# Windowed attention on one Trainium2 core: softmax sums applied to the output tile instead of the probabilities

## The chip, the cores and the metric

The kernel runs on one core of one Trainium2 chip. The metric is the device time of one execution in microseconds (us). Engines: PE is TensorE (matmuls; PEld is its weight load, which overlaps them), DVE is VectorE, ACT is ScalarE, POOL is GpSimd, SP is SyncE, which issues most DMAs.

## The reference

Two blocks with residual connections on x of 4 x 1024 x 256 in float32: first a causal attention of 16 heads of 16, then a network of two layers, each with an attention of 8 heads of 64 over windows of 128 tokens and a gated feed-forward part. The part that matters here, for one layer:

```python
q, k, v = split(shift_token(x) @ wqkv)          # 8 heads of 64
q, k = rotary(l2norm(q) * qs, l2norm(k) * ksc)
# window w of 128 queries sees the keys of windows w-1 and w
sim = einsum('bhwid,bhwjd->bhwij', 8 * bq, bk)   # 128 x 256 per head and window
sim = where(mask, -max, sim)
attn = softmax(sim, axis=-1)
out = einsum('bhwij,bhwjd->bhwid', attn, bv)     # 128 x 64 per head and window
x = x + out @ wo
h = layernorm(shift_token(x)) @ w1 + b1
a, g = split(h)
x = x + (a * gelu(g)) @ w2 + b2
```

## The kernel before

The program has two stretches. `prepare`, `causal_attention` and `project_causal` compute the first attention; they end about 890 us into the span and the change does not touch them. `layers` computes the two layers as 8 passes (`it` = 0 to 7, layer times batch), each `attention(it)` followed by `feed_forward(it)`. All five engines have their own hand-written program with the same step counter, and they meet at semaphores (`Count.of(it, item)` is the value that stands for an item).

`attention` has 32 units `u`: window `w = u // 4`, and within a window 4 units of two heads. `place(u, h)` tells at which place (feature tile `p`, and `side`, upper or lower 64 partitions) a head lies. One unit goes through

- PE `scores` (L1322): q times k, two heads side by side into bank `s_ps[u % 2]`;
- DVE `mask_scores` (L1763): adds the band, negates, takes the row minimum, writes `p_sb`;
- ACT `exponentials` (L1535): exp in place in `p_sb`, row sums into `total`;
- DVE `invert_sums` (L1812), then `scale_probs` (L1818): the reciprocal of two sums, and two products that divide the two heads' probabilities in `p_sb`;
- PE `turn_probs` (L1387): transposes the 128 x 128 blocks into `pt_ps`, so that keys lie on partitions; it waits for `scaled`;
- ACT `copy_probs` (L1551): `pt_ps` to `p_t`;
- PE `values` (L1402), once for two units: with v as the 128 x 64 stationary operand, the output with features on partitions goes to `o_ps`. One head's 64 features use one half of the array's columns (`tile_position=(0, side * HD2)`), and the two halves alternate;
- ACT `copy_output` (L1559), once for a window: `o_ps` to `o_t`.

PE's program for step u is, in this order: `scores(u)`, `turn_probs(u-2)`, in the first two steps of a window `turn(w+1, 0)` and `turn(w+1, 1)` (L1308, the rotated q and k of the next window, transposed into `turn_ps`, from where ACT's `copy_turned`, L1529, takes them), in the other steps a third of `project(w+3)` (L1285, q, k, v of a later window), and at even steps `values`. `project_out` (L1334) multiplies `o_t` by wo: for the first half of the tokens at steps 21 and 22, for the second half at the start of `feed_forward`. DVE also does the squares' sums (L1734), the unit vectors (L1740), the products with the sines (L1754) and, late in a pass, `residual` (L1773), the statistics and the normalisation of the first half. POOL does the rotation's cosines and its sum (L1670, L1675) and the powers of the norms. ACT's `scale_norm` (L1543) stands at step 30.

In passes 5 to 7 (`it > B`) the previous pass's last output tiles are transposed back on the way: `final_tiles` (L1298) at PE's steps 2 and 6 into `turn_ps`, and `final_add` (L1806) on DVE at steps 3 and 7.

## Time and profile before

| | us |
|---|---|
| median of 3 runs | 2465.59 (2464.23 to 2466.78) |
| the profiled execution: its own time | 2466.81 |
| the profiled execution: its span | 2465.1 |
| one pass of `layers` (1317 to 1508) | 191 |

The span is what the hardware profiler saw on the core. What lies around it (1.7 us) belongs to the time, too. Of the span, some 890 us are the first attention, and 8 passes of some 191 us follow. Busy time of an engine counts its instructions; a matmul's record lasts longer than the time after which the next one can start, so for PE the starts in the order of time tell more than the durations. fp32 matmuls have two records each, transposes one.

### The profile page before, as it was taken

To read this page: it belongs to the slowest core of one execution; us is meant where nothing else is said; L and a number is where in the kernel's file an instruction comes from. 1 tells how busy PE (TensorE), PEld (TensorE's weight loads), DVE (VectorE), ACT (ScalarE), POOL (GpSimd) and SP (SyncE) were. 2 spreads that over 40 slices of the span, in tenths; PEclk is the share of its full clock that TensorE was granted. 3 is DMA by queue.
4 is the path that set the end of the run, shared out by engine and by line. 5 is a ranking of instruction groups with operands and counts; after the bars stand their busy time and mean duration, and the time that the engine had idled before them with its cause. 6 is when DMAs were issued, how large, how long until landed. Compare 5 with 4: busy or idle time off the path is not lost.

```text
span 2465.1 us, 35578 instructions
## 1 busy us (share of the span) xinstructions
PE 2167.1 (88%) x11712; PEld 1249.6 (51%) x11712; DVE 1578.2 (64%) x3994; ACT 1193.7 (48%) x2840; POOL 819.1 (33%) x711
## 2 busy tenths in 40 slices
PE   5653899999987749999999999999999999999998
PEld 3331333333332515665665665665566566566556
DVE  5653677777773527647747747756856855855864
ACT  1210666666665315535535545644544643644552
POOL 2321321111131335235325325425415514514520
PEclk9885899999999969999999999999999999999999
DMA  5459344555521621000000000102000010010000
GB/s 149 135 145 159 106 68 69 78 78 78 102 91 23 181 86 74 18 26 9 18 26 9 18 26 9 46 26 99 18 18 18 18 35 18 18 35 18 18 1 26
DMA packets 130692, 135.22 MB, mean 55 GB/s; under 512 B 50556, under 2 KB 107472, under 8 KB 129488
## 3 DMA queue, kind: packets, MB, share of 16 engines
q1 hardware_dynamic: 129936, 124.05, 21.6%
q0 software_dynamic: 576, 8.91, 0.9%
q8 instruction: 96, 1.57, 0.3%
q14 instruction: 84, 0.69, 0.1%
HBM read 81.80 MB, written 50.86 MB: 54 GB/s over the span
## 4 chain that ended last, share of the span: by engine, by line
PE 41%; DVE 12%; issue 5%; ACT 3%; POOL 2%; DMA 0%; DVEq 0%; SPq 0%; POOLq 0%
PE qkv_ps L1285 9%; PE s_ps L1322 6%; PE qkv_ps L1334 5%; PE pt_ps L1387 4%; PE o_ps L1402 4%; DVE p_sb L1818 3%; PE s_ps L1441 3%; PE s_ps L1374 3%; DVE p_sb L1763 2%; PE o_ps L1441 1%; PE pt_ps L1441 1%; POOL inv_norm L1662 1%; PE pt_ps L1374 1%; PE o_ps L1374 1%; PE turn_ps L1308 1%
## 5 line engine op out<-in xcount | busy, mean ns | idle before, releaser
L735 DVE TENSOR_REDUCE piece_negmax<-s_ps 128x1 f32<-128x512 f32 (+3 forms) x768 | 372.9, 550 | 135.9 <-PE s_ps L591 133.6
L691 ACT ACTIVATE probs<-st_ps 128x512 f32<-128x512 f32 (+3 forms) x768 | 330.0, 495 | 180.8 <-PE st_ps L606 178.5
L1285 PE MATMUL qkv_ps<-w_qkv,x_in 128*128 128x512 f32 x768 | 366.6, 611 | 24.8 <-SPq L1224 17.0
L1818 DVE TENSOR_SCALAR p_sb<-p_sb,inv_total 128x256 f32<-128x256 f32 (+1 forms) x512 | 305.1, 636 | 39.4 <-DVE inv_total L1812 13.5
L1551 ACT COPY p_t<-pt_ps 128x512 f32<-128x512 f32 (+1 forms) x256 | 143.4, 560 | 327.2 <-PE pt_ps L1387 326.9
L588 PE MATMUL s_ps<-k_stack,q_stack 96*128 96x512 bf16 (+3 forms) x768 | 247.8, 343 | 43.1 <-DMA v_sb<-v_scratch 28.7
L1322 PE MATMUL s_ps<-k_t,q_t 64*128 64x256 f32 (+1 forms) x1024 | 270.9, 389 | 0.6 <-DVE gate L1850 0.5
L1535 ACT ACTIVATE p_sb<-p_sb,negmax 128x256 f32<-128x256 f32 (+1 forms) x512 | 249.4, 490 | 41.8 <-DVE negmax L1763 40.2
L1763 DVE CUSTOM_DVE_ANT_0 p_sb<-s_ps,band 128x256 f32<-128x256 f32 (+1 forms) x512 | 186.8, 401 | 124.3 <-PE s_ps L1322 117.5
L606 PE MATMUL st_ps<-q_stack,k_stack 98*128 98x512 bf16 (+3 forms) x768 | 231.8, 332 | 13.8 <-ACT probs L691 11.2
L1670 POOL TENSOR_TENSOR rot_c<-qn,turn_by 128x512 f32<-128x512 f32 x128 | 165.8, 1316 | 180.8 <-PE turn_ps L1308 152.6
L1322 PEld LDWEIGHTS s_ps<-k_t,q_t 64*128 64x128 f32 x1024 | 163.5, 186 | 118.7 <-issue 80.1
L810 POOL TENSOR_SCALAR_AFFINE_SELECT probs<-probs 128x512 f32<-128x512 f32 x128 | 81.2, 634 | 415.2 <-ACT probs L691 415.2
L1285 PEld LDWEIGHTS qkv_ps<-w_qkv,x_in 128*128 128x128 f32 x768 | 138.7, 195 | 154.5 <-issue 140.3
L1387 PE MATMUL pt_ps<-ident,p_sb 128*128 128x128 f32 x960 | 162.8, 290 | 43.2 <-ACT p_t L1551 21.8
L1662 POOL TENSOR_TENSOR inv_norm<-sum_sq,neg_half 128x16 f32<-128x16 f32 x64 | 187.5, 2929 | 5.3
L1675 POOL TENSOR_TENSOR rot_c<-rot_c,rot_s 128x1024 f32<-128x1024 f32 x64 | 155.2, 2426 | 98.4 <-DVE rot_s L1754 98.4
L1387 PEld LDWEIGHTS pt_ps<-ident,p_sb 128*128 128x128 f32 x960 | 101.4, 142 | 127.1 <-issue 63.8
L620 PE MATMUL o_ps<-probs,v_sb 128*32 128x512 f32 (+3 forms) x1536 | 163.6, 498 | 1.1 <-POOL probs L810 0.7
L606 PEld LDWEIGHTS st_ps<-q_stack,k_stack 98*128 98x128 bf16 x768 | 68.9, 98 | 152.6 <-ACT probs L691 112.2
L1374 PE MATMUL s_ps<-hn_t,w_ffn 128*128 128x512 f32 (+1 forms) x528 | 142.1, 420 | 0.0
L1402 PE MATMUL o_ps<-p_t,v_tok 128*64 128x128 f32 x1920 | 133.1, 279 | 5.4 <-ACT p_t L1551 5.4
(136 smaller groups left out, 3335.1 us busy)
## 6 DMA issues: line engine op xcount, KB each, us to landing
qk_scratch<-parts SPq DMA_DIRECT2D x64, 192.0 KB, 2.8
q_stack<-qk_scratch SPq DMA_DIRECT2D x96, 128.0 KB, 6.9
k_stack<-qk_scratch SPq DMA_DIRECT2D x96, 128.0 KB, 7.1
w_ffn<-ffn_weights POOLq DMA_DIRECT2D x4, 2176.0 KB, 12.1
v_scratch<-v_out SPq DMA_DIRECT2D x32, 256.0 KB, 2.5
v_sb<-v_scratch SPq DMA_DIRECT2D x16, 512.0 KB, 10.1
x_in<-xt_scratch SPq DMA_DIRECT2D x16, 512.0 KB, 3.6
turn_by<-in_rotary SPq DMA_DIRECT2D x8, 1024.0 KB, 5.2
```

What stands on the lines that cost most here:

```text
L588: mm = pe.matmul(s_ps[i % 3][:, 0:kw], q_stack[0:STK, slot, h, qt * P:(qt + 1) * P], k_stack[0:STK, slot, h, k0:k0 + kw], start=True, stop ...
L606: pe.matmul(st_ps[i % 3][:, q0:CH], k_stack[0:STK + SHIFT, slot, h, kt * P:(kt + 1) * P], q_stack[0:STK + SHIFT, slot, h, c * CH + q0:(c + ...
L691: act.activation(probs[:, n % 3, h, q0:CH], st_ps[i % 3][:, q0:CH], ACT.Exp).then_inc(exp_done.sem, 1)
L735: dve.tensor_reduce(piece_negmax[:, h, i % NP:i % NP + 1], s_ps[i % 3][:, 0:kw], AX.X, ALU.max, negate=True).then_inc(piece_done.sem, 1)
L1285: mm = pe.matmul(qkv_ps[:, part * CH:(part + 1) * CH], x_in[:, k, w * P:(w + 1) * P], w_qkv[:, k, part * INNER:(part + 1) * INNER], start= ...
L1322: mm = pe.matmul(s_ps[u % 2][:, (h + 1) * PW - ((w + 1) * P - k0):(h + 1) * PW], q_t[r, w % 2, p, :], k_t[r, p, k0:(w + 1) * P], start=Tru ...
L1374: mm = pe.matmul(up_pair(c, j)[bank][0:rows, :], w_up(w, k, tile)[:, 0:rows], hn_t[:, h, k, :], start=n == 0, stop=n == len(steps) - 1)
L1387: mm = pe.transpose(pt_ps[:, (h * 2 + kt) * P:(h * 2 + kt + 1) * P], p_sb[:, u % 4, h, kt * P:(kt + 1) * P], ident[:, :])
L1402: mm = pe.matmul(o_ps[side * HD2:(side + 1) * HD2, p * P:(p + 1) * P], v_sb[:, (w - 1 + kt) % VR, head * HD2:(head + 1) * HD2], p_t[:, u % ...
L1535: act.activation(p_sb[:, u % 4, h, k0:PW], p_sb[:, u % 4, h, k0:PW], ACT.Exp, scale=-1.0, bias=negmax[:, u % 4, h:h + 1], accum_out=total[ ...
L1763: dve.tensor_tensor_reduce(p_sb[:, u % 4, h, k0:PW], s_ps[u % 2][:, h * PW + k0:(h + 1) * PW], band[:, k0:PW], 1.0, BIG, ALU.add, ALU.min, ...
L1818: dve.tensor_scalar(p_sb[:, u % 4, h, k0:PW], p_sb[:, u % 4, h, k0:PW], inv_total[:, u % 4, h:h + 1], None, ALU.mult).then_inc(scaled.sem, 1)
```

## The change

The probabilities are no longer divided. `turn_probs` waits for `exp_done` alone and transposes the exponentials as they are. The sums of all eight heads of a window are kept (`total[P, 2, PAIRS, 2]`), and one reciprocal a window inverts them (128 x 8). PE's new `spread_sums(w)` then lays the inverses out as the output lies, features on partitions: eight matmuls with one inverse column, repeated 64 times, as the stationary operand and the identity as the moving one, into the bank `turn_ps`, with the same `tile_position` as `values`. DVE's new `scale_output(w)` multiplies the 128 x 512 tile of `o_t` by it in place. `project_out` waits for `o_scaled` in the place of `o_copied`. Since `turn_ps` is now in use until `scale_output` has read it, `turn(w, 0)` waits for `o_scaled(w - 3)`; `spread_sums(w)` waits for ACT's copy of the k of window w+2 out of that bank; and the `final_tiles` of passes 5 to 7 move from steps 2 and 6 to steps 1 (into `o_ps`) and 2 (into `turn_ps`).

```diff
-        total = sb("total", [P, 4, 2])
-        inv_total = sb("inv_total", [P, 4, 2])
+        total = sb("total", [P, 2, PAIRS, 2])
+        inv_total = sb("inv_total", [P, 2, PAIRS, 2])
...
             def turn(it, w, j):
-                if it > B and 1 <= w <= 3 and j == 0:
-                    pe.wait_ge(fin_added.sem, fin_added.of(it - 1 - B, w))
+                if it > B and w == 2 and j == 0:
+                    pe.wait_ge(fin_added.sem, fin_added.of(it - 1 - B, 3))
+                if w >= 3 and j == 0:
+                    pe.wait_ge(o_scaled.sem, o_scaled.of(it, w - 3))
...
-                pe.wait_ge(o_copied.sem, o_copied.of(it, (c + 1) * WPC - 1))
+                pe.wait_ge(o_scaled.sem, o_scaled.of(it, (c + 1) * WPC - 1))
...
                 def turn_probs(u):
                     w = u // PAIRS
-                    pe.wait_ge(scaled.sem, scaled.of(it, 2 * u + 1))
+                    pe.wait_ge(exp_done.sem, exp_done.of(it, 2 * u + 1))
...
+                def spread_sums(w):
+
+                    pe.wait_ge(inv_sum.sem, inv_sum.of(it, w))
+                    pe.wait_ge(turn_copied.sem, turn_copied.of(it, 2 * min(w + 2, NT - 1) + 1))
+                    for p in range(PAIRS):
+                        for side in range(2):
+                            mm = pe.matmul(turn_ps[side * HD2:(side + 1) * HD2, p * P:(p + 1) * P],
+                                           inv_total[:, w % 2, p, side:side + 1].to_broadcast([P, HD2]), ident[:, :],
+                                           start=True, stop=True, tile_position=(0, side * HD2))
+                    mm.then_inc(spread.sem, 1)
+
                 def values(g):
                     w = 2 * g // PAIRS
+                    if it > B and g == 0:
+                        pe.wait_ge(fin_added.sem, fin_added.of(it - 1 - B, 2))
...
-                    if it > B and u in (2, 6):
-                        pe.wait_ge(turn_copied.sem, turn_copied.of(it, 2 * w + 3))
-                        final_tiles(it - 1, 1, w, turn_ps)
+                    if it > B and u == 1:
+                        final_tiles(it - 1, 1, 0, o_ps)
+                    if it > B and u == 2:
+                        pe.wait_ge(turn_copied.sem, turn_copied.of(it, 3))
+                        final_tiles(it - 1, 1, 1, turn_ps)
+                    if u >= PAIRS + 2 and (u - 2) % PAIRS == 0:
+                        spread_sums((u - 2) // PAIRS - 1)
...
             def exponentials(it, u):
...
+                if u % PAIRS == 0:
+                    act.wait_ge(inv_sum.sem, inv_sum.of(it, w - 2))
...
-                def invert_sums(u):
-                    dve.wait_ge(exp_done.sem, exp_done.of(it, 2 * u + 1))
-                    dve.reciprocal(inv_total[:, u % 4, :], total[:, u % 4, :]).then_inc(inv_sum.sem, 1)
-
-                def scale_probs(u):
-                    k0 = 0 if u // PAIRS else WIN
-                    wait_apart(dve, passed, inv_sum.sem, inv_sum.of(it, u))
-                    for h in range(2):
-                        dve.tensor_scalar(p_sb[:, u % 4, h, k0:PW], p_sb[:, u % 4, h, k0:PW],
-                                          inv_total[:, u % 4, h:h + 1], None, ALU.mult).then_inc(scaled.sem, 1)
-
-                for u in range(UNITS + 1):
+                def invert_sums(w):
+                    dve.wait_ge(exp_done.sem, exp_done.of(it, 2 * (w + 1) * PAIRS - 1))
+                    if w >= 2:
+                        dve.wait_ge(spread.sem, spread.of(it, w - 2))
+                    dve.reciprocal(inv_total[:, w % 2], total[:, w % 2]).then_inc(inv_sum.sem, 1)
+
+                def scale_output(w):
+                    dve.wait_ge(spread.sem, spread.of(it, w))
+                    dve.wait_ge(o_copied.sem, o_copied.of(it, w))
+                    window = o_t[:, :, w * P:(w + 1) * P]
+                    dve.tensor_tensor(window, turn_ps[:, :].rearrange("p (h t) -> p h t", h=PAIRS), window, ALU.mult)\
+                       .then_inc(o_scaled.sem, 1)
+
+                for u in range(UNITS + 4):
...
-                    if u:
-                        invert_sums(u - 1)
-                        scale_probs(u - 1)
-                    if it > B and u in (3, 7):
-                        final_add(it - 1, 1, w, turn_ps)
+                    if u >= PAIRS + 1 and (u - 1) % PAIRS == 0:
+                        invert_sums((u - 1) // PAIRS - 1)
+                    if u >= PAIRS + 3 and (u - 3) % PAIRS == 0:
+                        scale_output((u - 3) // PAIRS - 1)
+                    if it > B and u in (1, 3):
+                        final_add(it - 1, 1, u // 2, turn_ps if u // 2 else o_ps)
```

PE, steps 8 to 10 of a pass, where window 2 begins; `L1387` is `turn_probs`, `L1308` `turn`, `L1285` `project`. Before, then changed (there `turn_probs` is L1390, `turn` L1311, `project` L1286, `values` L1418, and L1400 is `spread_sums`):

```order
L1387 MATMUL pt_ps<-ident,p_sb 128x128 x4
L1308 MATMUL turn_ps<-ident,rot_c 128x128 x4
L1285 MATMUL qkv_ps<-w_qkv,x_in 128x512 x2
L1322 MATMUL s_ps<-k_t,q_t 128x256 x2
L1387 MATMUL pt_ps<-ident,p_sb 128x128 x4
L1285 MATMUL qkv_ps<-w_qkv,x_in 128x512 x2
L1402 MATMUL o_ps<-p_t,v_tok 64x128 x8
```

```order
L1390 MATMUL pt_ps<-ident,p_sb 128x128 x4
L1311 MATMUL turn_ps<-ident,rot_c 128x128 x4
L1286 MATMUL qkv_ps<-w_qkv,x_in 128x512 x2
L1325 MATMUL s_ps<-k_t,q_t 128x256 x2
L1390 MATMUL pt_ps<-ident,p_sb 128x128 x4
L1400 MATMUL turn_ps<-ident,inv_total 64x128 x8
L1286 MATMUL qkv_ps<-w_qkv,x_in 128x512 x2
L1418 MATMUL o_ps<-p_t,v_tok 64x128 x8
```

Eight matmuls of the shape of `values` stand between the transposes of the probabilities and a third of a projection, once a window; nothing else on PE changes its place.

PE at the end of a pass's attention, where the last window's values are followed by the second half's `project_out` (L1334, L1337). Before, then changed:

```order
L1374 MATMUL s_ps<-hn_t,w_ffn 128x512 x12
L1402 MATMUL o_ps<-p_t,v_tok 64x128 x8
L1387 MATMUL pt_ps<-ident,p_sb 128x128 x4
L1402 MATMUL o_ps<-p_t,v_tok 64x128 x8
L1334 MATMUL qkv_ps<-o_t,w_out 128x512 x8
```

```order
L1377 MATMUL s_ps<-hn_t,w_ffn 128x512 x12
L1418 MATMUL o_ps<-p_t,v_tok 64x128 x8
L1390 MATMUL pt_ps<-ident,p_sb 128x128 x4
L1400 MATMUL turn_ps<-ident,inv_total 64x128 x8
L1418 MATMUL o_ps<-p_t,v_tok 64x128 x8
L1337 MATMUL qkv_ps<-o_t,w_out 128x512 x8
```

Here the new matmuls stand directly ahead of values.

DVE in the steps of window 1 and 2; `L1812` and `L1818` are `invert_sums` and `scale_probs`, and in the changed kernel L1836 and L1842 are `invert_sums` and `scale_output`, L1785 `mask_scores`, L1756 `sums`. Before, then changed:

```order
L1734 TENSOR_REDUCE sum_sq<-squares 128x16
L1763 ISA p_sb,negmax<-s_ps,band 128x256
L1763 ISA negmax 128x1
L1763 ISA p_sb,negmax<-s_ps,band 128x256
L1763 ISA negmax 128x1
L1812 RECIPROCAL inv_total<-total 128x2
L1818 TENSOR_SCALAR p_sb<-p_sb,inv_total 128x256 x2
```

```order
L1756 TENSOR_REDUCE sum_sq<-squares 128x16
L1785 ISA p_sb,negmax<-s_ps,band 128x256
L1785 ISA negmax 128x1
L1785 ISA p_sb,negmax<-s_ps,band 128x256
L1785 ISA negmax 128x1
L1842 TENSOR_TENSOR o_t<-turn_ps,o_t 128x4x128
```

The reciprocal and the two products that stood behind every unit's masks are gone; one product of 128 x 512 stands behind the masks of each window's last unit, and one reciprocal behind those of the second.

## Rows read from the trace of the kernel before

**Rows 1.** The page: busy time of the engines, and PE's clock in 40 slices.
```profile
PE 2167.1 (88%) x11712; PEld 1249.6 (51%) x11712; DVE 1578.2 (64%) x3994; ACT 1193.7 (48%) x2840; POOL 819.1 (33%) x711
...
PEclk9885899999999969999999999999999999999999
```

**Rows 2.** Busy time by stretch: a pass; the next one's attention; its feed-forward part.
```profile
core 0: us, PE busy (x) PEld busy (x) DVE busy (x) ACT busy (x) POOL busy (x), PEclk, DMA share, GB/s
1317.00:1508.00 191.00, 181.41 (x916) 115.63 (x916) 126.36 (x333) 97.43 (x235) 75.36 (x52) 1.00 0.05 17
1508.00:1624.00 116.00, 108.56 (x636) 67.21 (x636) 88.83 (x267) 68.45 (x188) 46.62 (x30) 1.00 0.08 27
1624.00:1699.00 75.00, 72.85 (x280) 48.43 (x280) 37.95 (x66) 28.95 (x48) 29.45 (x24) 1.00 0.07 25
```

**Rows 3.** PE in order of time, fifth pass: start us, us, what; idle before and releaser in brackets.
```profile
1519.72 0.66 PE L1402 MATMUL o_ps<-p_t,v_tok 128*64 128x128 f32 x8
1520.31 1.13 PE L1322 MATMUL s_ps<-k_t,q_t 64*128 64x256 f32 x4
...
1533.78 1.09 PE L1402 MATMUL o_ps<-p_t,v_tok 128*64 128x128 f32 x16
1534.81 1.13 PE L1322 MATMUL s_ps<-k_t,q_t 64*128 64x256 f32 x4
...
1539.85 0.66 PE L1387 MATMUL pt_ps<-ident,p_sb 128*128 128x128 f32 x4
1540.35 1.88 PE L1285 MATMUL qkv_ps<-w_qkv,x_in 128*128 128x512 f32 x4
...
1600.13 0.66 PE L1387 MATMUL pt_ps<-ident,p_sb 128*128 128x128 f32 x4
1600.71 1.09 PE L1402 MATMUL o_ps<-p_t,v_tok 128*64 128x128 f32 x16
```

**Rows 4.** Who PE waited for, 800 us to the end: us in total, times, longest.
```profile
PE pt_ps L1387 <- ACT p_t L1551: 21.8, 8, 2.7
PE pt_ps L1387 <- DVE p_sb L1818: 17.8, 35, 1.3
```

**Rows 5.** The same of PE's weight loads, from 890 us on.
```profile
PEld pt_ps L1387 <- issue: 63.8, 142, 2.9
PEld pt_ps L1387 <- DVE p_sb L1818: 63.2, 113, 2.9
```

**Rows 6.** PE's weight loads in order of time, fifth pass.
```profile
1539.85 0.42 PEld L1387 LDWEIGHTS pt_ps<-ident,p_sb 128*128 128x128 f32 x4 [0.52 <-DVE p_sb L1818]
...
1542.16 0.85 PEld L1402 LDWEIGHTS o_ps<-p_t,v_tok 128*64 128x64 f32 x16 [0.76 <-issue]
1543.18 0.73 PEld L1322 LDWEIGHTS s_ps<-k_t,q_t 64*128 64x128 f32 x4 [0.17 <-issue]
1544.24 0.42 PEld L1387 LDWEIGHTS pt_ps<-ident,p_sb 128*128 128x128 f32 x4 [0.33 <-DVE p_sb L1818]
```

**Rows 7.** Instructions of single lines: duration ns min/median/max, first and last start.
```profile
L1818 DVE TENSOR_SCALAR p_sb<-p_sb,inv_total x512: 273/352/1936, 930.9 to 2392.6; 128x256 f32<-128x256 f32 x150, 128x128 f32<-128x128 f32 x21
...
L1773 DVE TENSOR_TENSOR x_mid<-qkv_ps,x_in x32: 676/688/693, 1012.9 to 2408.5; 128x512 f32<-128x512 f32 x32
...
L1402 PEld LDWEIGHTS o_ps<-p_t,v_tok x1920: 132/137/137, 944.2 to 2400.2; 128*64 128x64 f32 x192
```

**Rows 8.** End of the fifth pass's attention, in order of time, PE and ACT.
```profile
1611.34 1.09 PE L1402 MATMUL o_ps<-p_t,v_tok 128*64 128x128 f32 x16
...
1612.92 0.57 ACT L1559 COPY o_t<-o_ps 128x512 f32<-128x512 f32 x1
...
1616.79 0.63 PE L1387 MATMUL pt_ps<-ident,p_sb 128*128 128x128 f32 x4 [2.72 <-ACT p_t L1551]
...
1622.47 1.09 PE L1402 MATMUL o_ps<-p_t,v_tok 128*64 128x128 f32 x16 [0.68 <-ACT p_t L1551]
...
1623.61 0.58 ACT L1559 COPY o_t<-o_ps 128x512 f32<-128x512 f32 x1 [1.19 <-PE o_ps L1402]
```

**Rows 9.** ACT's copy of a turned k in window 6, same pass, in order of time.
```profile
1600.21 0.57 ACT L1529 COPY k_t<-turn_ps 128x512 f32<-128x512 f32 x1
```

More of the change, by code:

```diff
@@ L1135, in layers @@
         exp_done = count("exp_done2", 2 * UNITS)
-        inv_sum = count("inv_sum", UNITS)
-        scaled = count("scaled", 2 * UNITS)
+        inv_sum = count("inv_sum", NT, 2)
+        spread = count("spread", NT)
+        o_scaled = count("o_scaled", NT)
         pt_ready = count("pt_ready", UNITS, 4)
@@ L1531, in exponentials @@
             def exponentials(it, u):
-                k0 = 0 if u // PAIRS else WIN
+                w, k0 = u // PAIRS, 0 if u // PAIRS else WIN
+                if u % PAIRS == 0:
+                    act.wait_ge(inv_sum.sem, inv_sum.of(it, w - 2))
                 for h in range(2):
@@ L1536, in exponentials @@
                                    bias=negmax[:, u % 4, h:h + 1],
-                                   accum_out=total[:, u % 4, h:h + 1]).then_inc(exp_done.sem, 1)
+                                   accum_out=total[:, w % 2, place(u, h)[0], place(u, h)[1]:place(u, h)[1] + 1]).then_inc(exp_done.sem, 1)
             def scale_norm(it, c):
@@ L1725, in _ @@
         def _(dve):
-            for c in (qn_ready, sin_ready, s_masked, mid_ready, hn_t_split, hidden_ready, hidden_split, out_ready):
+            for c in (qn_ready, sin_ready, s_masked, inv_sum, mid_ready, hn_t_split, hidden_ready, hidden_split, out_ready):
                 dve.sem_inc(c.sem, c.credit)
@@ L1809, in attention @@
             def attention(it):
-                def invert_sums(u):
-                    dve.wait_ge(exp_done.sem, exp_done.of(it, 2 * u + 1))
-                    dve.reciprocal(inv_total[:, u % 4, :], total[:, u % 4, :]).then_inc(inv_sum.sem, 1)
-                def scale_probs(u):
-                    k0 = 0 if u // PAIRS else WIN
-                    wait_apart(dve, passed, inv_sum.sem, inv_sum.of(it, u))
-                    for h in range(2):
-                        dve.tensor_scalar(p_sb[:, u % 4, h, k0:PW], p_sb[:, u % 4, h, k0:PW],
-                                          inv_total[:, u % 4, h:h + 1], None, ALU.mult).then_inc(scaled.sem, 1)
-                for u in range(UNITS + 1):
+                def invert_sums(w):
[10 more added lines that the diff above has]
+                for u in range(UNITS + 4):
                     w, p = u // PAIRS, u % PAIRS
```

## The prediction

> **What bounds the kernel now.** I read the page first: PE is busy 88% of the span, DVE 64%, ACT 48% [rows 1]. A share over the whole span says little, so next come the stretches. In one pass of the layers PE is busy 181.4 of 191 us, DVE 126.4 and ACT 97.4; in the attention part alone PE has 108.6 of 116 us and DVE 88.8; the granted clock is 1.00, the 2.4 GHz level [rows 2]. The question is whether that busy time is real or only long records. PE in order of time answers it: each group of matmuls starts when the streaming of the one before it ends, and what a group takes until the next starts goes with its number of records. Eight records of values take 0.59 us (1519.72 to 1520.31), sixteen take 1.03 (1533.78 to 1534.81) [rows 3]. So PE is the limit of the 8 passes, and what the others do counts only where PE waits for them.
>
> Then the waits. PE's own list has two entries of size that concern the attention: 21.8 us for ACT's copy of the turned probabilities (8 times, once a pass) and 17.8 us for the products of L1818, which this change removes [rows 4]. The second one is understated there, since the record of a matmul covers a short wait. The list of the weight loads has it as 63.2 us over 113 times [rows 5]. But that is overstated: a load of L1387 stands idle 0.33 us behind the scores even where nothing holds it up, as at 1544.24, and the loss is what goes beyond it, 0.19 of the 0.52 at 1539.85 [rows 6].
>
> **The change, part by part.** The sum is made against the profiled execution, 2466.8 us, which lies 1.2 us above the median of 2465.6.
>
> Removed: 512 products on DVE and 256 small reciprocals. The products take 0.35 us in the median but up to 1.94 [rows 7]. DVE's time itself is worth nothing, for PE covers it (126 of 191 us in a pass [rows 2]); were DVE the bound, it would be worth some 300 us. The worth is in PE's wait: 63.2 us less 113 x 0.33 = 37.3 gives 25.9. One of the 113 is the longest, 2.9 us, and that is the stall of each pass that ACT's copy causes ([rows 4] has it 8 times, longest 2.7), so 2.6 go off: **-23.3 us**. What is late next is the exponential of the same unit, which was done before the reciprocal could start, so I let nothing remain of this wait. Bounds: PE's own list, 17.8, and the undiminished 25.9.
>
> Added on PE: 64 times (8 windows, 8 passes) eight matmuls with a 128 x 64 stationary operand and 128 moving columns. That is the shape, the type and the alternation of halves of values (L1402), so its rows give the price. Eight records more cost 1.03 - 0.59 = 0.44 us, so sixteen stream for 0.88, and 0.15 of the 1.03 is the step from this form to another one. The step into it costs, too: from transposes to values 0.58 us (1600.13 to 1600.71), from transposes to a projection 0.50 (1539.85 to 1540.35), a difference of 0.08 [rows 3]. In windows 0 to 4 the new group stands between transposes and 512-column matmuls and pays both: 5 x 8 x 1.11 = 44.4 us. In windows 5 and 6 values follow at once and the steps are paid already: 2 x 8 x 0.88 = 14.1. In window 7 it stands ahead of the values that wait 0.68 us for ACT's copy today [rows 8] and fills that wait: 8 x (0.88 - 0.68) = 1.6. Together **+60.1 us**. Bounds: 64 x 0.88 less the 5.4 of the filled wait, 51, and 64 x 1.11, 71. Not shown by any row is the stationary operand that repeats one element 64 times; its nearest row is the load of the 64 columns of v, 0.137 us [rows 7], and I take it as equal.
>
> The Trainium skill (TensorE: Matmul & The Clock Gate, Part 3: Packing small matmuls) says that a weight load overlaps running matmuls only where its row group differs, and the row group is the same for all eight here. By that rule the sum would be a good deal higher; it is a rival below. In the trace sixteen loads of L1402 stand within 0.85 us, each 0.137 long, beside matmuls that run on [rows 6, 7], so the trace does not agree.
>
> Added on DVE: 64 products of 128 x 512 with one operand in PSUM; the nearest row, L1773, has 0.69 us for that size [rows 7]. They are 44 us against 305 removed and lie beside PE, with one exception: at the end of the attention the second half's `project_out` must now wait for the product as well as for ACT's copy, which ends at 1624.2 there [rows 8] and directly releases it. 0.69 and a semaphore's 0.1: 8 x 0.8 = **+6.4 us**. For the first half, 4 steps lie between, so nothing. Bounds 4 and 10.
>
> The waits that are new. `spread_sums` comes two steps behind the window's last exponentials, so the reciprocal (some 0.15 us) is there. It also waits for ACT's copy of k out of the bank. That copy is over before in windows 0 to 4, where a projection of 1.8 us lies in between. In window 5 it is not: the copy runs 1600.21 to 1600.78, and the transposes in front end at about 1600.6 [rows 3, 9]: 8 x 0.2 = **+1.6 us**. Behind it on PE stand values and all the rest. `turn(w, 0)` waits for the product of window w-3, one step of DVE earlier; with the projection in that step it is there in time, and I put it at nothing up to window 5. For ACT, the wait for the reciprocal of w-2 is three steps old when it comes: nothing. DVE's `scale_output` holds the next masks back if PE's group or ACT's copy is late; both come a step earlier, and DVE has 300 us less to do.
>
> The stall of 2.72 us at the end of each attention [rows 8] is ACT's: copies and the normalisation's four operations follow each other from 1612.92 on. PE's new group in window 6 holds the values back by 0.88 us, ACT's copy by about 0.5 (it starts 1612.92, the values end at about 1612.4), so the stall swallows 0.4: **-3.2 us**, bounds 0 and -7.
>
> The moved `final_tiles`: same count of transposes in 3 passes, the same DVE sums, earlier by a step or four. PE's step 1 now waits for the previous pass's last output, for which step 2 waits anyway. Nothing; 1 us a pass if that cover fails. No DMA is added; the last store of a pass may start a few us earlier, with the queues nearly idle (0.05 of their time [rows 2]).
>
> Sum: -23.3 + 60.1 + 6.4 + 1.6 - 3.2 = +41.6. 2466.8 + 41.6 = 2508.4 for the profiled execution, and 2507 for the median.
>
> **The rivals.** *PE has room.* If the busy PE is only an effect of long records, the 64 groups hide and the gain stays: 2466.8 - 23.3 - 3.2 + 6.4 + 1.6 = 2448, faster. Its place is PE between the transposes and the projection in windows 0 to 4. It decides from the point where a group costs PE less than 26.5 / 64 = 0.4 us instead of 0.9 to 1.1. For it speaks that PE's loads are busy only 115.6 of 191 us [rows 2]. Against it: sixteen records of the very same form push the next group back by 1.03 us, with no wait in between [rows 3]. The Trainium skill (Perfetto Trace Analysis, Identifying the Most-Contended Engine) calls matmul busy time a bad measure of headroom and wants the busy share of the weight loads, which is 61% in a pass; by this page PE would have room and the time would be that of this rival. The starts in rows 3 don't agree.
>
> *The halves do not run side by side.* If the repeated column or the shared bank made the two column halves follow each other, a record would cost the 0.11 us of a 128-column transpose (0.42 us for four loads [rows 6]) instead of 0.055, and the group 0.88 more: 64 x 0.88 = 56 us, 2564. The same form in values speaks against it. *The loads don't overlap at all*, the mechanism of the page above: 16 x 0.137 = 2.2 us more each, 64 x 2.2 = 140, 2648. Against it the same rows.
>
> *The bank becomes a wait.* `turn_ps` passes through PE, ACT and DVE twice a window. In windows 6 and 7, where no projection lies in between, `turn(w, 0)` would come before masks (0.9 us), copy (0.57) and product (0.69) of the step before are through, and lose up to 1 us: 2 x 8 x 1 = 16, 2523. For it speaks that in that stretch PE already waited for DVE now and then; against, that DVE has lost the products that made it late.
>
> **How the numbers follow.** The forecast's case has 0.80, the bank 0.08, the halves 0.05, the loads 0.02, room on PE 0.05. The forecast's own bounds, all together, are 51 + 4 + 0 - 25.9 - 7 = +22 and 71 + 10 + 5 - 17.8 - 0 = +68: 2487 to 2533 for the median, which takes in the bank. Outside are 0.12 and the tails; I keep 2487 to 2532. A measurement of this kernel can tell 0.2% (4.9 us) from nothing. Faster by more than that is the room on PE alone, of whose 0.05 I give 0.01 to a half-hidden group that ends level; another 0.01 of the forecast ends there too. Faster 0.04, same 0.02, slower 0.94.
>
> **What the changed profile would show.** PE: 1024 more records, a group of sixteen with 128*64 at the new line, about 1.0 to 1.1 us from its start to the next group's; PE's busy time up by some 55 us. The waits of the transposes for DVE's products gone, and none for ACT's exponentials of like size in their place. `project_out` idle about 1.6 us behind DVE once a pass in the place of 0.8 behind ACT. A pass of 196 us instead of 191. DVE's busy time down by some 270 us with no effect. The prediction is wrong if a pass is not longer, if the group takes over 1.5 us, or if `turn` or the new matmuls have a list of waits of over 10 us.

## The result, and the profile after

The changed kernel takes 2507.35 us, the median of 4 runs (2506.64 to 2510.49), beside 2465.27 for the kernel before: a ratio of 1.0173, 95% interval 1.0155 to 1.0190. It is slower by 42 us. The forecast was 2507 and slower. Two executions of the experiments below (8286.04 us of the kernel with the product out of PSUM, 2673.39 us of the one with the group next to the values) ran at mean granted clocks of 0.55 and 0.82, where the others had 0.95 to 0.96, and are left out of every median here.

The page of the changed kernel, the lines that answer to [rows 1], and DVE's lines of the groups of instructions (the line engine op, out<-in, count | busy us, mean ns | idle before it and its releasers):

```profile
span 2505.3 us, 36971 instructions
...
PE 2231.9 (89%) x12736; PEld 1303.7 (52%) x12736; DVE 1401.5 (56%) x3354; ACT 1197.7 (48%) x2840; POOL 830.5 (33%) x711
```

```profile
L1776 DVE TENSOR_TENSOR rot_s<-qn,turn_by 128x256 f32<-128x256 f32 x256 | 199.1, 837 | 0.3
...
L1842 DVE TENSOR_TENSOR o_t<-turn_ps,o_t 128x512 f32<-128x512 f32 x64 | 44.0, 687 | 61.8 <-ACT o_t L1581 61.8
```

PE has 1024 records more, two for each of the 512 new matmuls, and is busy 65 us longer (forecast: some 55). DVE is busy 177 us less (1578.2 in [rows 1]), and the kernel is slower all the same. The span grew by 40.2 us, from 2465.1 to 2505.3.

The fourth pass of the changed kernel (`it` = 3; what stands ahead, [rows 3] and [rows 8] too, calls this same pass the fifth), PE in order of time; it answers to [rows 3] and [rows 8] (L1390 `turn_probs`, L1400 `spread_sums`, L1286 `project`, L1418 `values`, L1377 `up`, L1337 `project_out`):

```profile
1588.79 0.66 PE L1390 MATMUL pt_ps<-ident,p_sb 128*128 128x128 f32 x4
1589.37 1.09 PE L1400 MATMUL turn_ps<-ident,inv_total 128*64 128x128 f32 x16
1590.40 1.98 PE L1286 MATMUL qkv_ps<-w_qkv,x_in 128*128 128x512 f32 x4
1592.31 1.09 PE L1418 MATMUL o_ps<-p_t,v_tok 128*64 128x128 f32 x16
...
1621.40 0.66 PE L1390 MATMUL pt_ps<-ident,p_sb 128*128 128x128 f32 x4
1622.20 1.09 PE L1400 MATMUL turn_ps<-ident,inv_total 128*64 128x128 f32 x16
1623.10 1.07 PE L1418 MATMUL o_ps<-p_t,v_tok 128*64 128x128 f32 x16
...
1638.49 0.63 PE L1390 MATMUL pt_ps<-ident,p_sb 128*128 128x128 f32 x4 [2.30 <-ACT p_t L1573]
1638.87 4.59 PE L1377 MATMUL s_ps<-hn_t,w_ffn 128*128 128x512 f32 x12
1643.39 1.09 PE L1418 MATMUL o_ps<-p_t,v_tok 128*64 128x128 f32 x16
1644.42 0.66 PE L1390 MATMUL pt_ps<-ident,p_sb 128*128 128x128 f32 x4
1645.00 1.09 PE L1400 MATMUL turn_ps<-ident,inv_total 128*64 128x128 f32 x16
1645.93 1.04 PE L1418 MATMUL o_ps<-p_t,v_tok 128*64 128x128 f32 x16
1648.54 7.11 PE L1337 MATMUL qkv_ps<-o_t,w_out 128*128 128x512 f32 x16 [1.57 <-DVE o_t L1842]
```

Read the starts. From the transposes to the projection it is now 1.61 us (1588.79 to 1590.40), before 0.50 (1539.85 to 1540.35, [rows 3]): 1.11 for a group. The projection behind it takes 1.91 up to the values instead of 1.81 (1540.35 in [rows 3] to 1542.16 in [rows 6]), another 0.10. In window 5 the group starts 0.80 behind the transposes instead of 0.58, so it waits 0.22. The stall for ACT, in which PE stands idle behind ACT's copy of the turned probabilities, is 2.30 (before 2.72), and `project_out` starts 2.61 behind the last values (before 1.87, 1622.47 in [rows 8] to the start in this line of the kernel before):

```profile
1624.34 7.10 PE L1334 MATMUL qkv_ps<-o_t,w_out 128*128 128x512 f32 x16 [0.78 <-ACT o_t L1559]
```

Who PE waited for, and then the same of its weight loads, which answer to [rows 4] and [rows 5]:

```profile
PE pt_ps L1390 <- ACT p_t L1573: 18.4, 8, 2.3
...
PE qkv_ps L1337 <- DVE o_t L1842: 12.6, 8, 1.6
```

```profile
PEld pt_ps L1390 <- issue: 85.3, 209, 2.5
...
PEld pt_ps L1390 <- ACT p_sb L1557: 10.6, 32, 0.3
```

The 63.2 us behind DVE's products are gone. What took their place, the exponentials, has 32 entries of at most 0.33 us each, which is the idle time that stands there without any wait.

Summing all differences of start times between the two fourth passes (from the transposed q of one pass to that of the next) gives this, in us:

| | forecast, a pass | measured |
|---|---|---|
| 5 groups in windows 0 to 4, and what follows each | 5 x 1.11 = 5.55 | 5 x 1.21 = 6.05 |
| groups of windows 5, 6, 7 | 1.08, 0.88, 0.20 | 1.12, 0.92, 0.18 |
| `project_out` behind the product | 0.80 | 0.74 |
| ACT's stall | -0.40 | -0.42 |
| transposes behind scores (the wait for the products) | -2.9 | -3.77 |
| transposes of the normalised tile | 0 | -0.41 |
| the first matmuls of `up`, at another clock | 0 | +1.58 |
| the rest | 0 | +0.6 |

The sum of the measured column is 6.6 in this pass and 5.0 without the clock. Eight times 5.0 is 40, the difference of the spans. The clock's row is not part of the change: over all eight passes the same twelve matmuls take 32.5 us in the changed kernel's profiled execution and 34.2 in the other's. Nor is this pass the mean for the waits: over eight passes the transposes behind the scores start 26.1 us earlier in all (3.3 a pass), those of the normalised tile 3.1.

### The profile page after: what moved, and what is told of

The parts are those of the page before. It is cut to its first block, busy times and chain, and to the rows that moved or that the text cites. A ratio compares the mean times of both kernels' runs of the same rounds, so it can differ in the third digit from the quotient of the medians.

```text
span 2505.3 us, 36971 instructions
## 1 busy us (share of the span) xinstructions
PE 2231.9 (89%) x12736; PEld 1303.7 (52%) x12736; DVE 1401.5 (56%) x3354; ACT 1197.7 (48%) x2840; POOL 830.5 (33%) x711
## 4 chain that ended last, share of the span: by engine, by line
PE 53%; DVE 5%; ACT 3%; POOL 3%; issue 1%; DMA 0%; SPq 0%; DVEq 0%; POOLq 0%
PE qkv_ps L1286 13%; PE s_ps L1325 9%; PE pt_ps L1390 5%; PE o_ps L1418 5%; PE qkv_ps L1337 5%; PE s_ps L1377 3%; PE s_ps L1461 3%; PE turn_ps L1400 3%; POOL inv_norm L1684 2%; PE turn_ps L1311 2%; PE pt_ps L1377 2%; PE pt_ps L1461 1%; PE o_ps L1461 1%; PE o_ps L1377 1%; DVE hidden L1881 1%
## 5 line engine op out<-in xcount | busy, mean ns | idle before, releaser
L1286 PE MATMUL qkv_ps<-w_qkv,x_in 128*128 128x512 f32 x768 | 368.6, 613 | 25.0 <-SPq L1225 17.5
L1785 DVE CUSTOM_DVE_ANT_0 p_sb<-s_ps,band 128x256 f32<-128x256 f32 (+1 forms) x512 | 187.4, 403 | 250.3 <-PE s_ps L1325 240.5
L1692 POOL TENSOR_TENSOR rot_c<-qn,turn_by 128x512 f32<-128x512 f32 x128 | 178.4, 1414 | 194.2 <-PE turn_ps L1311 164.4
L1286 PEld LDWEIGHTS qkv_ps<-w_qkv,x_in 128*128 128x128 f32 x768 | 138.0, 194 | 160.0 <-issue 145.5
L1776 DVE TENSOR_TENSOR rot_s<-qn,turn_by 128x256 f32<-128x256 f32 x256 | 199.1, 837 | 0.3
L1756 DVE TENSOR_REDUCE sum_sq<-squares 128x16 f32<-128x1024 f32 x64 | 77.9, 1217 | 185.1 <-ACT squares L1536 185.1
L1390 PE MATMUL pt_ps<-ident,p_sb 128*128 128x128 f32 x960 | 161.6, 288 | 18.4 <-ACT p_t L1573 18.4
L1390 PEld LDWEIGHTS pt_ps<-ident,p_sb 128*128 128x128 f32 x960 | 100.5, 141 | 97.7 <-issue 85.3
L1702 POOL TENSOR_SCALAR var_eps<-mean_var 128x4 f32<-128x4 f32 x16 | 5.4, 336 | 417.5 <-DVE mean_var L1808 417.5
```

The costliest lines, as they stand in the source:

```text
L1286: mm = pe.matmul(qkv_ps[:, part * CH:(part + 1) * CH], x_in[:, k, w * P:(w + 1) * P], w_qkv[:, k, part * INNER:(part + 1) * INNER], start= ...
L1390: mm = pe.transpose(pt_ps[:, (h * 2 + kt) * P:(h * 2 + kt + 1) * P], p_sb[:, u % 4, h, kt * P:(kt + 1) * P], ident[:, :])
L1692: ins = pool.tensor_tensor(heads(rot_c, j), heads(qn, j), turn_by[:, w, 2 * j, :].unsqueeze(1) .to_broadcast([P, H2, HD2]), ALU.mult)
L1776: dve.tensor_tensor(dst[:, :, o], src[:, :, i], turn_by[:, w, 2 * j + 1, o].unsqueeze(1) .to_broadcast([P, H2, half]), ALU.mult).then_inc( ...
L1785: dve.tensor_tensor_reduce(p_sb[:, u % 4, h, k0:PW], s_ps[u % 2][:, h * PW + k0:(h + 1) * PW], band[:, k0:PW], 1.0, BIG, ALU.add, ALU.min, ...
```

## The experiments

The kernel before was run again beside the experiments (medians of 2465.26 to 2466.25 us), and each ratio is taken against those runs. The changed kernel was not, so "less than the changed kernel" is always against 2507.35. Where two profiled executions are compared, the stretch ahead of the layers, which no edit touches, differs too: the first `scores` start between 920.1 and 928.7 us.

### The gain alone: the division taken away

In the kernel before, nothing is divided and the output stays unscaled:

```diff
-                    pe.wait_ge(scaled.sem, scaled.of(it, 2 * u + 1))
+                    pe.wait_ge(exp_done.sem, exp_done.of(it, 2 * u + 1))
...
-                    if u:
-                        invert_sums(u - 1)
-                        scale_probs(u - 1)
```

> The kernel before without the division: no products, no reciprocals, the transposes wait for the exponentials (the output is left undivided). Theory (PE is the limit, the products are worth only PE's wait for them): the fifth pass of the changed kernel shows the transposes 3.8 us and the transposes ahead of the normalised tile 0.4 us earlier, so 8 x 4.2 = 33 us less than before, 2432; by the prediction's term, 23 less, 2442. Rival (DVE's 305 us bound something beside that): more than 50 us less, under 2415. Rival (the gain is nothing, the exponentials are waited for instead): 2460 or more.

Measured: 2438.42 us (4 runs, 2435.70 to 2439.24), ratio 0.9888 (0.9875 to 0.9901), 28 us less than before. Both rivals are out: the whole division, 305 us of products and 40 of reciprocals on DVE, was worth 28 us. Of the two sizes given neither was met; 28 lies between the prediction's 23 and the 33 of the theory, which took the fourth pass for the mean of all. The changed kernel lies 69 us above this one, and that is what its substitute costs.

### The same with DVE's load kept

As above, but every reciprocal and product is still formed:

```diff
+                    if it or u:
+                        dve.wait_ge(scaled.sem, scaled.of(it, 2 * u - 1))
                     for h in range(2):
-                        dve.tensor_scalar(p_sb[:, u % 4, h, k0:PW], p_sb[:, u % 4, h, k0:PW],
+                        dve.tensor_scalar(gate[:, u % 4, h * PW + k0:(h + 1) * PW], p_sb[:, u % 4, h, k0:PW],
```

> The same, but DVE still forms every reciprocal and every product, into slots of gate that nobody reads, so only PE's wait for them is gone and DVE's load stays. Theory: within 5 us of e1. Rival (it is DVE's load, with products of up to 1.9 us, that holds the masks back): at least half of the way back from e1 to the kernel before, 2450 or more.

Measured: 2451.47 us (5 runs, 2450.16 to 2457.57), ratio 0.9948 (0.9936 to 0.9960). That is 13 us above the kernel without the products, where my theory allowed 5, so the theory failed. The rival's 2450 or more is met, its half of the way back nearly (13 of 28). The products take as long as before (621 ns in the mean for 128 x 256, before 624), so the load is the same, and it has a worth of its own. It does not show behind the masks, where the rival had it: over all passes the transposes behind the scores start as early as without the division. PE's waits of this kernel show where it is lost:

```profile
PE qkv_ps L1351 <- DVE hn L1793: 7.5, 8, 1.3
```

The normalised tile comes late from DVE, once a pass, and PE waits for it. Between the same groups of one pass, the transposes of that tile start 1.06 us later than in the kernel without products, 8.5 us in 8 passes. In the fourth pass another 1.0 us stands at the turned q and k of a window and what follows them. How the 28 us split depends on the order in which the two are taken away: the wait first gives 15, the load after it 13.

### Four matmuls of full width

DVE widens the inverses to 128 x 512 (into slots of `gate` that the attention does not use), and four matmuls lay them out without column halves:

```diff
+                    wait_apart(dve, passed, inv_sum.sem, inv_sum.of(it, w))
+                    dve.tensor_copy(heads(gate[:, 2 + w % 2, :]), inv_total[:, w % 2].rearrange("p a s -> p (a s)").unsqueeze(2)
+                                    .to_broadcast([P, H2, HD2])).then_inc(widened.sem, 1)
...
-                        for side in range(2):
-                            mm = pe.matmul(turn_ps[side * HD2:(side + 1) * HD2, p * P:(p + 1) * P],
-                                           inv_total[:, w % 2, p, side:side + 1].to_broadcast([P, HD2]), ident[:, :],
-                                           start=True, stop=True, tile_position=(0, side * HD2))
+                        mm = pe.matmul(turn_ps[:, p * P:(p + 1) * P], gate[:, 2 + w % 2, p * P:(p + 1) * P], ident[:, :],
+                                       start=True, stop=True)
```

> The changed kernel with the inverses widened to 128 x 512 by DVE and laid out by four matmuls of full width instead of eight in column halves: the same 0.87 us of streaming (8 records of 0.107), but no change of the array's form. Theory (in windows 0 to 4 a group costs 1.11 us up to the next and 0.10 more in what follows, 0.34 of it for the change of form): 40 x 0.34 = 13 us less than the changed kernel, 2494. Rival (the form is free and only streaming counts, or the repeated column is what costs): 2507, or under 2480.

Measured: 2491.47 us (4 runs, 2490.92 to 2492.51), ratio 1.0106 (1.0092 to 1.0121), 16 less than the changed kernel. The theory's 13 is near it: in the fourth pass the starts give 1.4 us, 11 in eight, and in the profiled executions the twelve matmuls behind ACT's stall take 29.3 us instead of 32.5, which is the clock.

### The group moved next to the values

Two lines change their place, nothing else:

```diff
-                    if u >= PAIRS + 2 and (u - 2) % PAIRS == 0:
-                        spread_sums((u - 2) // PAIRS - 1)
                     if p >= 1 and w + AHEAD < NT:
                         project(it, w + AHEAD, p - 1)
...
+                    if u >= PAIRS + 2 and (u - 2) % PAIRS == 0:
+                        spread_sums((u - 2) // PAIRS - 1)
                     if u >= 4 and u % 2 == 0:
                         values((u - 4) // 2)
```

> The changed kernel with its eight column-half matmuls moved behind the projection, directly ahead of the values of the same step, which have the same form. Nothing else. Theory (0.34 us of the 1.21 in windows 0 to 4 is the change of form): 40 x 0.34 = 13.6 less, and 0.2 in window 5 covers nothing new, so 2493 to 2494, as the full-width form gave by another way. Rival (the 0.34 belongs to the matmuls themselves): 2507.

Measured: 2494.06 us (the median of four runs, 2492.03 to 2496.20), ratio 1.0116 (1.0095 to 1.0137), 13.3 less than the changed kernel; the theory said 13.6. PE in the fourth pass:

```profile
1574.94 1.09 PE L1400 MATMUL turn_ps<-ident,inv_total 128*64 128x128 f32 x16
1575.87 1.04 PE L1418 MATMUL o_ps<-p_t,v_tok 128*64 128x128 f32 x16
```

The group now costs 0.93 up to the values. The matmuls are the same and in the same number, so the 0.3 us belong to the change of the array's form: transposes and projections use it whole, these matmuls and values use its column halves. The Trainium skill (TensorEngine Tiling (Array Packing), Key Properties) says that changing the mode drains the engine. The trace is in line with it: 0.15 us for leaving, 0.08 for entering and 0.10 in the first full-width matmuls behind it. That a drain is what takes this time, no run shows.

### Every group twice

```diff
+                    for again in range(2):
                         for p in range(PAIRS):
                             for side in range(2):
```

> The changed kernel with every group of eight laid out twice in a row, the same values into the same place (sixteen matmuls a window). Theory (PE's streaming, 0.875 us for sixteen records, is paid in every window): 64 x 0.875 = 56 us more, 2563. Rival (a good part of the added group lies in time that PE has anyway): under 2545. Rival (the group costs more than its records, by loads that don't overlap): over 2580.

Measured: 2564.80 us (4 runs, 2562.07 to 2566.89), ratio 1.0405 (1.0387 to 1.0423), 57 more than the changed kernel; the theory said 56. PE in the fourth pass:

```profile
1609.18 1.97 PE L1401 MATMUL turn_ps<-ident,inv_total 128*64 128x128 f32 x32
1611.08 1.98 PE L1286 MATMUL qkv_ps<-w_qkv,x_in 128*128 128x512 f32 x4
```

This settles that PE had no room: from the group to the projection it is 1.90 us instead of 1.03, so 64 groups more are paid in full at 0.87 us each, 56 us; the last microsecond is within the spread of the runs.

### Transposes instead of matmuls

As the full-width form, with `pe.transpose` in the place of `pe.matmul`, which has one record instead of two:

```diff
-                        mm = pe.matmul(turn_ps[:, p * P:(p + 1) * P], gate[:, 2 + w % 2, p * P:(p + 1) * P], ident[:, :],
-                                       start=True, stop=True)
+                        mm = pe.transpose(turn_ps[:, p * P:(p + 1) * P], gate[:, 2 + w % 2, p * P:(p + 1) * P],
+                                          ident[:, :])
```

> The same widened inverses, laid out by four PE transposes (one record each, 0.107 us). Theory: windows 0 to 4 cost 0.43 instead of 1.21, 40 x 0.78 = 31 less; windows 5 and 6 0.43 instead of 0.92, 16 x 0.49 = 8 less; window 7 1 to 2 less; from 2507 to 2467 (2462 to 2472). Rival (the price is the waits around the bank turn_ps, not PE's time): 2500 or more.

Measured: 2476.62 us (6 runs, 2468.73 to 2481.54), ratio 1.0043 (1.0028 to 1.0059). The rival is out: 31 us are gone. But 2467 was missed by 10. In the profiled execution (2472.8) part of the difference is TensorE's clock. Here are three stretches around the end of the fourth pass's attention, the columns being busy us and, after POOL, the granted clock. The twelve matmuls behind the stall follow, of the kernel before in its fourth and fifth pass, and of the changed one in its fourth:

```profile
core 0: us, PE busy (x) PEld busy (x) DVE busy (x) ACT busy (x) POOL busy (x), PEclk, DMA share, GB/s
...
1621.00:1625.00 4.00, 4.00 (x14) 2.99 (x12) 0.63 (x2) 0.62 (x2) 0.00 (x0) 0.68 0.01 4
1625.00:1630.00 5.00, 3.28 (x41) 2.56 (x40) 0.69 (x1) 2.00 (x3) 0.00 (x0) 1.00 0.01 2
1630.00:1637.00 7.00, 6.91 (x12) 2.98 (x13) 0.69 (x1) 1.14 (x2) 0.00 (x0) 0.76 0.00 0
```

```profile
1617.20:1620.10 2.90, 2.90 (x15) 2.13 (x12) 0.78 (x3) 0.91 (x3) 0.00 (x0) 1.00 0.03 6
...
1808.50:1813.60 5.10, 5.10 (x14) 3.81 (x12) 0.78 (x3) 0.71 (x3) 0.00 (x0) 0.53 0.00 0
```

```profile
1638.90:1643.30 4.40, 4.40 (x14) 3.26 (x12) 0.20 (x1) 0.90 (x3) 0.00 (x0) 0.61 0.01 4
```

The twelve matmuls behind ACT's stall take 2.94 us at a granted clock of 1.00, the 2.4 GHz level, and 3.9 to 5.4 in the runs here when it falls to 1.2 GHz for a part of them or for nearly all. In the kernel with transposes `project_out`, behind the second wait of the pass (1.57 us), runs at the lower clock too, and takes 8.23 us up to the next group (6.54 in the changed kernel: 1648.54 to 1655.08). That is 1.7 us, in each of five of the eight passes, 8.5 in all. Between the same groups of two passes of the profiled executions, transposes save 4.8 us beside this, 38 in eight, against my 40; 38 less 8.5 is 30, and the medians differ by 31. So the transposes saved what was forecast, and the clock took the difference. That the clock took as much in the executions without a profile is not shown.

### The wait for the product taken away

In the changed kernel DVE writes its product where nobody reads it, and the output stays unscaled:

```diff
-                pe.wait_ge(o_scaled.sem, o_scaled.of(it, (c + 1) * WPC - 1))
+                pe.wait_ge(o_copied.sem, o_copied.of(it, (c + 1) * WPC - 1))
...
-                    window = o_t[:, :, w * P:(w + 1) * P]
+                    window = gate[:, w % 4, :].rearrange("p (h t) -> p h t", h=PAIRS)
```

> The changed kernel, but DVE writes its products into slots of gate that nobody reads, and the output projection waits for ACT's copy as before (the output is left undivided). It takes away the one wait at the end of each attention. Theory: that wait costs 0.74 us a pass, 8 x 0.74 = 6 less, 2501. Rival (scaling the output delays PE in other places, too): 2495 or less. Rival (the wait is covered): 2507.

Measured: 2499.85 us (4 runs, 2494.18 to 2502.76), ratio 1.0139 (1.0119 to 1.0159), 7.5 less than the changed kernel. Its `project_out` starts 0.80 us earlier behind the values, 6.4 us in 8 passes. The spread of its runs (8.6 us) covers the last microsecond.

### The product taken out of PSUM

On top of the transposes, ACT copies the inverses and DVE multiplies out of `o_ps`:

```diff
-                    act.wait_ge(pv_done.sem, pv_done.of(it, (w + 1) * PAIRS // 2 - 1))
-                    if w == 0:
-                        act.wait_ge(wo_ready.sem, wo_ready.of(it, -1))
-                    act.copy(o_t[:, :, w * P:(w + 1) * P], o_ps[:, :].rearrange("p (h t) -> p h t", h=PAIRS))\
+                    act.wait_ge(spread.sem, spread.of(it, w))
+                    act.wait_ge(o_scaled.sem, o_scaled.of(it, w - 2))
+                    act.copy(gate[:, w % 2, :], turn_ps[:, :])\
...
-                    dve.tensor_tensor(window, turn_ps[:, :].rearrange("p (h t) -> p h t", h=PAIRS), window, ALU.mult)\
+                    dve.tensor_tensor(window, o_ps[:, :].rearrange("p (h t) -> p h t", h=PAIRS),
+                                      gate[:, w % 2, :].rearrange("p (h t) -> p h t", h=PAIRS), ALU.mult)\
```

> The kernel with the four transposes, and the roles of the two tiles exchanged: ACT copies the inverses out of turn_ps, DVE multiplies the outputs by them straight out of o_ps into o_t, so the chain behind the last values is one step instead of two. Theory: 0.6 to 0.8 us less at the end of each attention, 5 to 6 us less than the kernel with the transposes, so 2471, or 2467 from its profiled run. Rival (the bank of the outputs is now free later and values wait): no gain, 2476 or more.

Measured: 2465.17 us (the median of eleven runs, 2461.43 to 2469.61), ratio 1.0003 (0.9993 to 1.0013). It is level with the kernel before: the cost of laying the sums out is down to what the division's removal brings. It is 11 us less than the kernel with transposes, where 5 to 6 were forecast. The shorter chain gives 0.62 a pass, 5 us, as forecast; the rest is the clock, for in the profiled executions `project_out` is at the full clock again in all passes, 1.7 us in each of five.

### Two of ACT's operations given to DVE, with the change and without

ACT's stall is the largest wait left. Of the four operations of `scale_norm` in the attention, the two that write the float32 half go to DVE:

```diff
+                    if c == 0:
+                        act.wait_ge(full_done.sem, full_done.of(it, k))
-                    for out in (full_t(k), hn_t[:, 0, k, :]):
+                    for out in (full_t(k), hn_t[:, 0, k, :])[0 if c else 1:]:
...
+                    if u == NORM_AT + 6:
+                        dve.wait_ge(back_ready.sem, back_ready.of(it, KD - 1))
+                        for k in range(KD):
+                            dve.tensor_scalar(full_t(k), ln_ps[k], ln_g[:, k:k + 1], ln_b[:, k:k + 1], ALU.mult,
+                                              ALU.add).then_inc(full_done.sem, 1)
```

> The kernel with transposes and the product out of PSUM, and in each attention two of the four operations of ACT's normalisation step (the float32 half of the tile, two of 0.66 us) go to DVE, which the change has freed. Theory: the stall of 2.3 us at the end of the attention shrinks by 1.3 to 1.5, 8 x 1.4 = 11 less than 2465, so 2454; if with it the half clock behind the stall goes, which costs 0 to 2.3 us a pass in the traces so far, up to 9 more, 2445. Rival (DVE is late with the masks of the last unit instead): 2460 or more. Rival (the clock falls all the same): 2454.

> The kernel before with the same two operations moved from ACT to DVE and nothing else, so DVE still divides the probabilities. If the move works as well without the change: 11 to 20 less than 2465, 2445 to 2454, and the change's freed DVE is no part of it. Rival (DVE is too full at that place, its products and the normalisation make the transposes wait): 2458 or more.

Measured: with the change (on top of the product out of PSUM) 2457.44 us (10 runs, 2447.19 to 2463.15), ratio 0.9964 (0.9949 to 0.9978). Without it, 2462.16 us (12 runs, 2456.15 to 2464.90), ratio 0.9982 (0.9971 to 0.9993). The first one lies below both kernels, by 8 us where 11 to 20 were forecast; the second one meets the number of its rival (2458 or more). PE of the first one at the end of the fourth pass's attention, and then PE's waits of the second one:

```profile
1615.08 0.63 PE L1393 MATMUL pt_ps<-ident,p_sb 128*128 128x128 f32 x4 [0.95 <-ACT p_t L1576]
1616.49 3.05 PE L1380 MATMUL s_ps<-hn_t,w_ffn 128*128 128x512 f32 x12 [0.78 <-DVE hn_t L1827]
```

```profile
PE pt_ps L1389 <- DVE p_sb L1824: 31.1, 42, 1.7
```

With the change the stall falls from 2.3 to 0.95 us, but 0.78 of it come back as a wait for DVE's subtraction, which now comes behind that; and the clock still falls in every other pass (4.4 to 4.5 us for the twelve matmuls in passes 1, 3, 5 and 7, 3.0 in the rest). Without the change the stall is 1.69, and it is DVE's products that PE waits for. From the transposes ahead of the stall to the values behind it, a pass at the full clock takes 6.69 us before and 6.50 with the move; on top of the product out of PSUM 6.29 and 5.98. So the move alone is worth 0.19 and 0.31 us a pass, 1.5 and 2.5 in eight, and the medians' 3.7 and 7.7 us are more than that; in the profiled executions this stretch is 4.2 and 6.7 us shorter in all, and what goes beyond 1.5 and 2.5 there is the clock. The two intervals overlap, too. That the freed DVE makes the move worth more is at most a microsecond by the traces, and not shown by the times.

## Why the prediction was right

The sign, the size and the mechanism of the cost held; that the size came out to a microsecond is in part luck, as said below. *What bounds the kernel* held: 64 groups more cost their 56 us of streaming again, in full. *The group's price*, taken from values, was 1.11 us up to the next group, as read; the repeated column, for which there was no row, costs nothing of its own (its loads take 0.132 to 0.137 us, as those of v). The 0.10 that a projection takes longer behind a change of form was missed, 0.5 us a pass. *The tail* (0.8 forecast, 0.74 and 0.80 found; the semaphore's 0.1 in it stood on no row, and no run shows it by itself), *window 5's wait* (0.2, 0.22), *the last window's filled wait* (0.20, 0.18) and *the shrunk stall* (-0.4, -0.42) held each.

*The gain* was too small: -23.3 us forecast, -28 by the kernel without the division. Two things were off. The wait for the products, taken from the list of weight loads, was 26.1 us and not 23.3. And I wrote that DVE's time itself is worth nothing, for PE covers it; the kernel with the products set aside shows that this step failed. There PE no longer waits for a product, and still 13 of the 28 us are lost, most of them (8.5) at the normalised tile, which DVE makes too late; in the changed kernel that tile is ready 3.1 us earlier in all, a term that the forecast did not have. The cost was too small as well: 64.9 us forecast (60.1 + 6.4 + 1.6 - 3.2), 69 found, 4 of the difference in the projections that take 0.10 longer. The two errors of 4 to 5 us stand against each other, so the sum of 41.6 met the measured 42 by luck. DVE's busy time was to fall by some 270 us, and fell by 177; the reason is below.

Of the rivals, *PE has room* fell with the doubled groups. (Its threshold was miscounted: with the other terms in, a group would have had to cost less than 18.5 / 64 = 0.3 us, not 0.4, for the kernel to be faster.) With it fell the headroom that the busy share of the loads seems to give. The Trainium skill (Perfetto Trace Analysis, Identifying the Most-Contended Engine) wants TensorE's headroom judged by that share, 61% in a pass; here 64 added groups cost their streaming in full at that share, so the trace does not agree. *The halves one after the other* and *the loads that don't overlap* fell with the 1.02 us between starts. *The bank as a wait* fell too: no line of `turn` or of the new matmuls has a wait for DVE's product. Some lists of these lines do pass the 10 us that I named as a sign of being wrong, and none is such a wait: `turn` has one wait of 11.6 us for POOL and its loads stand idle 16.8 us with nothing that releases them, both as in the kernel before (11.6 and 17.0), and the new loads stand idle 12.2 us over 64 times, 0.19 each, again with no releaser.

## What to carry to other kernels

An engine that is busy all the time gives a price to every instruction that a change adds to it, and an instruction of the same form in the trace gives that price to a tenth of a microsecond; 345 us taken from an engine beside it were worth 28: about what the waits said (26), and a part of that hangs on what the engine's load holds back elsewhere, which a list of waits for the removed instructions does not show. Where something must go through a full PE, choose the form: four transposes cost 0.43 us where eight matmuls in column halves cost 1.2, of which 0.34 for changing the array's form twice. And where a second pass over a result is added, let it take the place of the copy, not come behind it.

## What the runs showed of the hardware that was not expected

**DVE's waiting for POOL moved from one line to another.** Before, in order of time, and then the changed kernel:

```profile
1581.64 2.54 POOL L1670 TENSOR_TENSOR rot_c<-qn,turn_by 128x512 f32<-128x512 f32 x2 [3.31 <-PE turn_ps L1308]
1581.78 2.56 DVE L1818 TENSOR_SCALAR p_sb<-p_sb,inv_total 128x256 f32<-128x256 f32 x2
...
1584.26 1.42 DVE L1754 TENSOR_TENSOR rot_s<-qn,turn_by 128x256 f32<-128x256 f32 x4
```

```profile
L1754 DVE TENSOR_TENSOR rot_s<-qn,turn_by 128x256 f32<-128x256 f32 x256 | 105.5, 470 | 0.1
```

```profile
1587.63 1.44 POOL L1692 TENSOR_TENSOR rot_c<-qn,turn_by 128x512 f32<-128x512 f32 x1
1587.88 1.82 DVE L1776 TENSOR_TENSOR rot_s<-qn,turn_by 128x256 f32<-128x256 f32 x2
```

Two products, of which one takes 0.35 us in the median, took 2.56 us while POOL's rotation ran, and the sines' products came behind it. With them gone, the sines' products (two inputs in SBUF) meet POOL, and take 0.84 us in the mean instead of 0.47: 94 of the freed microseconds of DVE went there. The Trainium skill (Advanced Engine Details and Errata, Mode Summary) says that the second SBUF port of VectorE is shared with GpSimd, and that GpSimd's instructions and VectorE's in a mode with two read ports block each other. The trace is in line with it for the removed products, though it does not tell their mode; for the sines' products it shows the same slowing (1.82 us for two).

**The clock falls behind a short stall, and not always.** After waits of 2.3 to 2.7 us the twelve matmuls of `up` took 2.94 us at a granted clock of 1.00 and up to 5.4 at one of 0.50, and the pattern over the passes differs from kernel to kernel: full in passes 2 to 4 before, low in 2 to 7 after. One pass can change by 2.3 us by this alone, and the runs of one kernel spread by up to 16 us (2447.19 to 2463.15, with the float32 half on DVE). So compare the same groups in the same pass, with the granted clock beside them, before a difference of a few us is put down to a change.
